# The last expert tile reaches the tokens by a matmul, the other tiles are gathered beside it, and x is stored in quarters

## What is computed

```python
# layer 0: top 1 of 8 experts, capacity int(512 / 8 * 1.25) + 1 = 81
slot = where(rank < capacity, top1 * capacity + rank, trash)
h = gelu(einsum('ecd,edf->ecf', eb, W1) + b1)
y = einsum('ecf,efd->ecd', h, W2) + b2
x = x + where(valid, y[slot], 0) * combine_w
# layer 1: top 2 of 8 experts, no capacity
for e in experts:
    w = sum(gates * (topi == e), -1)
    h = silu(x_ @ gate_w[e].T) * (x_ @ up_w[e].T)
    acc = acc + (h @ down_w[e].T) * w
x = x + acc          # x_ is the layer norm of x; out = x
```

## Time and profile before

| what | value |
|---|---|
| runs, us | 3772.26, 3777.95, 3777.58 (median 3777.58) |
| the profiled execution, us | 3774.2 |
| its span, us | 3772.9 |
| PE busy | 3586.1 us, 95% |
| DVE busy | 2570.7 us, 68% |
| ACT busy | 1928.2 us, 51% |
| POOL busy | 1774.7 us, 47% |
| experts of layer 0, first to last expert matmul | 1784.6 to 1978.3 |
| experts of layer 1, first to last expert matmul | 3225.7 to 3750.6 |

### The profile page before, as it was taken

The page is one execution under the profiler, slowest core; times in us unless marked ns, Lnnn a source line. Parts: engine busy times, 40 slices in busy tenths (PEclk is TensorE's granted clock), DMA queues, the critical chain, the costliest instruction groups (busy, mean ns, idle before and its releaser), DMA issues. The chain is left out here.

```text
span 3772.9 us, 46236 instructions
## 1 busy us (share of the span) xinstructions
PE 3586.1 (95%) x17924; PEld 2322.5 (62%) x17924; DVE 2570.7 (68%) x3488; ACT 1928.2 (51%) x1978; POOL 1774.7 (47%) x744
## 2 busy tenths in 40 slices
PE   8999999999999999988997999999999887999997
PEld 6788788655555555446873555555554475788886
DVE  3222344478878787546986787878775565899997
ACT  2122312366555555633981655555566322678775
POOL 2112112299999899700000989999998320100000
PEclk9999999999999999998996999999999998999999
DMA  7667765633333333045875333333330101899996
GB/s 280 201 201 237 240 207 195 203 78 86 89 77 88 90 84 74 20 149 191 358 316 161 75 86 79 81 90 90 77 88 23 51 1 44 346 380 374 371 379 249
DMA packets 235177, 613.76 MB, mean 163 GB/s; under 512 B 43169, under 2 KB 125121, under 8 KB 180689
## 3 DMA queue, kind: packets, MB, share of 16 engines
q1 hardware_dynamic: 196176, 537.40, 43.8%
q10 hardware_dynamic: 36864, 67.13, 4.8%
q0 software_dynamic: 1920, 6.29, 0.5%
HBM read 480.07 MB, written 130.58 MB: 162 GB/s over the span
## 5 line engine op out<-in xcount | busy, mean ns | idle before, releaser
L731 DVE TENSOR_REDUCE maxima<-psum 128x1 f32<-128x512 f32 x2048 | 1285.5, 682 | 341.6 <-PE psum L726 338.6
L840 ACT ACTIVATE pt<-psum 128x1024 f32<-128x1024 f32 x1024 | 1018.8, 1025 | 701.6 <-PE psum L751 696.1
L854 POOL TENSOR_TENSOR exp_sums<-pt 128x1024 f32<-128x1024 f32 x342 | 818.7, 2394 | 265.4 <-PE psum L767 131.5
L726 PE MATMUL psum<-ks,first_q 96*128 96x512 f32 x2048 | 814.3, 447 | 20.1 <-DMA first_q<-q_parts 10.1
L857 POOL TENSOR_TENSOR exp_sums<-exp_sums,pt 128x1024 f32<-128x1024 f32 x310 | 736.8, 2377 | 45.8 <-ACT pt L840 1.5
L726 PEld LDWEIGHTS psum<-ks,first_q 96*128 96x128 f32 x2048 | 393.9, 192 | 477.8 <-DVE maxima L731 323.7
L763 PE MATMUL psum<-pt,vs 128*32 128x512 f32 x4096 | 674.3, 598 | 4.6 <-DVE head_rows L868 2.3
L767 PE MATMUL psum<-exp_sums,constants 128*32 128x512 f32 x1408 | 670.2, 598 | 0.0
L751 PE MATMUL psum<-qs,ks 97*128 97x512 f32 x2048 | 649.4, 400 | 15.3 <-ACT pt L840 15.3
L1512 DVE TENSOR_TENSOR moe_cut<-moe_raw,moe_cut 128x2048 fp32r<-128x2048 f32 x244 | 557.3, 2290 | 57.0 <-ACT moe_cut L1508 51.4
L1508 ACT CAST moe_cut<-moe_raw 128x2048 fp32r<-128x2048 f32 x244 | 468.8, 1924 | 50.5 <-PE psum L97 47.8
(11 more groups left out here) (323 smaller groups left out, 4594.7 us busy)
## 6 DMA issues: line engine op xcount, KB each, us to landing
moe_raw<-in_moe_w SPq DMA_DIRECT2D x244, 1024.0 KB, 7.8
ks<-k_parts SPq DMA_DIRECT2D x384, 256.0 KB, 4.6
k_parts<-kparts ACTq DMA_DIRECT2D x256, 256.0 KB, 4.0
cx<-in_ctx SPq DMA_DIRECT2D x32, 1024.0 KB, 6.1
vs<-v_heads SPq DMA_DIRECT2D x32, 1024.0 KB, 5.2
v_heads<-vrow SPq DMA_DIRECT2D x28, 1024.0 KB, 5.1
late_context<-cparts SPq DMA_DIRECT2D x16, 512.0 KB, 12.2
late_parts<-late_context SPq DMA_DIRECT2D x16, 512.0 KB, 3.8
```

The source lines that it names most:

```text
L726: pe.matmul(self.c.bank[self.FIRST_BANK + k % 3], self.first_q[s][:, t * P:(t + 1) * P], self.ks[s][part][0:3 * DH, at:at + CHUNK], start= ...
L731: dve.tensor_reduce(self.maxima[:, h % 2, i % TT, i // TT:i // TT + 1], self.c.bank[self.FIRST_BANK + k % 3], X, ALU.max).then_inc(*self.f ...
L840: act.activation(self.pt[:, self.slot(h, b) + i:self.slot(h, b) + i + 2, :], self.c.psum[:, at:at + 2, :], ACT.Exp).then_inc(*self.exp.up())
L854: engine.tensor_tensor(to, self.pt[:, slot:slot + R, :], self.pt[:, slot + R:slot + 2 * R, :], ALU.add).then_inc(*signal.up())
```

## The change

- In tile 1, ahead of that tile's other work, DVE builds `spread`: for each of the four token tiles a 128x128 matrix with the token's weight at its place in the last tile, zero elsewhere (5 instructions in layer 0; 14 in layer 1, where a second matrix for the second choice is built in `select` and added).
- At the start of tile 2 PE transposes the four matrices into the bank of the turned tokens, and ACT copies them to `spread_t`.
- The last tile isn't stored to `y_slots`. Its rows there hold zeros, for which two more tiles of zeros are written early in the program (rows of tile 7, layer 0's last, and of tile 14, layer 1's last).
- POOL's gathers wait for the stores of the other tiles only, so they stand beside the last tile's work. DVE adds their rows ahead of the last tile's output in layer 0, behind its last operand work in layer 1.
- When the last tile's output is in `moe_yrow`, PE multiplies it by the four matrices, 128x512 each, into four banks, and DVE adds each to x.
- In layer 1 SP stores each quarter of x when it is ready. The wait for these stores stands ahead of the stage's barrier, not behind it.

```diff
@@ ProjectContext.loads_and_stores
-                for t in range(TT):
-                    sp.dma_start(S["y_slots"][(EXPERTS + t) * P:(EXPERTS + t + 1) * P, :], self.nothing[:]).then_inc(*self.zeros_out.up())
+                for tile in (EXPERTS - 1, *range(EXPERTS, EXPERTS + TT), TILES1 - 1):
+                    sp.dma_start(S["y_slots"][tile * P:(tile + 1) * P, :], self.nothing[:]).then_inc(*self.zeros_out.up())
@@ Experts
+    def spread_last_on_dve(self, dve):
+
+        for n in range(self.choices):
+            dve.tensor_scalar(self.place[:, n, :], self.slots[n], -float((self.tiles - 1) * P), None, ALU.add).then_inc(*self.placed.up())
+        dve.wait_ge(*self.placed.at(self.choices))
+        for t in range(TT):
+            dve.tensor_scalar(self.spread[:, t, :], self.c.iota[:], self.place[:, 0, t:t + 1], self.gate[0][:, t:t + 1], ALU.is_equal, ALU.mult).then_inc(*(self.placed if self.two else self.spread_made).up())
+        if self.two:
+            for t in range(TT):
+                dve.tensor_scalar(self.select[:, t, :], self.c.iota[:], self.place[:, 1, t:t + 1], self.gate[1][:, t:t + 1], ALU.is_equal, ALU.mult).then_inc(*self.spread_made.up())
...
+            for t in range(TT):
+                dve.tensor_tensor(self.spread[:, t, :], self.spread[:, t, :], self.select[:, t, :], ALU.add).then_inc(*self.spread_made.up())
@@ loads_and_stores
-        store(self.tiles - 1)
+        if self.out is not None:
+            for t in range(TT):
+                sp.wait_ge(*self.x_added.at(TT * self.choices + t + 1))
+                sp.dma_start(self.out[t * P:(t + 1) * P, :], self.x[:, t, :]).then_inc(*self.stored.up())
+            sp.wait_ge(*self.stored.all())
@@ on_pe, tile(j), at its start
+            if j == self.SPREAD_TILE:
+                pe.wait_ge(*self.spread_made.at(TT * self.choices))
+                for t in range(TT):
+                    last = pe.transpose(bank[self.X_BANK][:, t * P:(t + 1) * P], self.spread[:, t, :], c.ident[:])
+                last.then_inc(*self.spread_turned.up())
@@ on_pe, behind the last tile
+        pe.wait_ge(*self.y_done.at(self.tiles))
+        for t in range(TT):
+            pe.matmul(bank[t], self.spread_t[:, t, :], self.yrow[:, (self.tiles - 1) % 2, :], start=True, stop=True).then_inc(*self.last_made.up())
@@ on_act, at the start of a tile
+            if j == self.SPREAD_TILE:
+                act.wait_ge(*self.spread_turned.at(1))
+                act.copy(self.spread_t[:], bank[self.X_BANK].rearrange("p (t n) -> p t n", t=TT)).then_inc(*self.spread_copied.up())
@@ on_dve
+            if j + 1 == self.SPREAD_TILE:
+                self.spread_last_on_dve(dve)
...
+                if j + 1 == self.tiles:
+                    add_back()
                 dve.wait_ge(*self.used.at((j + 1) * self.pieces))
...
+        if self.two:
+            add_back()
+        for t in range(TT):
+            dve.wait_ge(*self.last_made.at(t + 1))
+            dve.wait_ge(*self.x_added.at((t + 1) * self.choices))
+            dve.tensor_tensor(self.x[:, t, :], self.x[:, t, :], bank[t], ALU.add).then_inc(*self.x_added.up())
@@ perceiver
-            nc.sync.dma_start(out.rearrange("(t p) d -> p t d", p=P), x[:]).then_inc(*stored.up())
-            nc.sync.wait_ge(*stored.all())
```

More of the change, by code:

```diff
@@ L1184, with __init__ @@
     AHEAD, RAW, CUT, JB = 3, 6, 4, FT // FB
-    EARLY_LOWS = 2
+    EARLY_LOWS, SPREAD_TILE = 2, 2
     TURN_BANK, X_BANK, OUT_BANK = 4, 6, 7
-    def __init__(self, c, A, S, x, l):
-        self.c, self.A, self.S, self.x, self.l = c, A, S, x, l
+    def __init__(self, c, A, S, x, l, out=None):
+        self.c, self.A, self.S, self.x, self.l, self.out = c, A, S, x, l, out
         self.two = l == 1
@@ L1206, in run @@
             self.select = c.sb(st, f"select{l}", [P, TT, P])
+            self.place = c.sb(st, f"place{l}", [P, 2, TT])
+            self.spread = c.sb(st, f"spread{l}", [P, TT, P])
+            self.spread_t = c.sb(st, f"spread_t{l}", [P, TT, P])
             self.norm = Normalize(c, st, self.x, f"ln_m{l}")
@@ L1237, in run @@
             self.first_ranked, self.selected = c.signals(st, "first_ranked selected")
+            self.placed, self.spread_made, self.spread_turned, self.spread_copied, self.last_made = c.signals(st, "placed spread_made spread_turned spread_copied last_made")
+            self.stored, = c.landings(st, "stored")
             if not self.two:
@@ L1283, in select_first_on_dve @@
             dve.tensor_scalar(self.select[:, t, :], self.c.iota[:], 1.0, self.first_rank[:, t:t + 1], ALU.add, ALU.is_equal).then_inc(*self.selected.up())
+    def spread_last_on_dve(self, dve):
[7 more added lines that the diff above has]
+                dve.tensor_scalar(self.select[:, t, :], self.c.iota[:], self.place[:, 1, t:t + 1], self.gate[1][:, t:t + 1], ALU.is_equal, ALU.mult).then_inc(*self.spread_made.up())
+            dve.wait_ge(*self.placed.at(self.choices + TT))
+            dve.wait_ge(*self.spread_made.at(TT))
+            for t in range(TT):
+                dve.tensor_tensor(self.spread[:, t, :], self.spread[:, t, :], self.select[:, t, :], ALU.add).then_inc(*self.spread_made.up())
     def plan_top1_on_dve(self, dve):
@@ L1321, in plan_top1_on_dve @@
         dve.tensor_copy(self.row_of[:, 0, :], slot).then_inc(*self.rows_known.up())
-        self.gate = [weight]
+        self.gate, self.slots = [weight], [slot]
     def plan_top2_on_dve(self, dve):
@@ L1382, in plan_top2_on_dve @@
         dve.tensor_copy(self.owneri[:], self.ownerf[:]).then_inc(*self.slot_made.up())
-        self.gate = [w1, w2]
+        self.gate, self.slots = [w1, w2], [slot1, slot2]
     def loads_and_stores(self, sp):
@@ L1497, in tile @@
                 if db == 1 and j + 1 < self.tiles:
+                    if j == self.SPREAD_TILE:
+                        pe.wait_ge(*self.spread_copied.at(1))
                     turn_x(j + 1)
@@ L1595, in leave_turned, with add_back @@
             dve.tensor_tensor(to, source, high.bitcast(F32), ALU.subtract).then_inc(*self.ht_low.up())
+        def add_back():
+            for t in range(TT):
+                dve.wait_ge(*self.y_back[t].at(self.choices))
+                for n in range(self.choices):
+                    if n:
+                        dve.wait_ge(*self.x_added.at(t * self.choices + n))
+                    dve.scalar_tensor_tensor(self.x[:, t, :], self.back(t, n), self.gate[n][:, t:t + 1], self.x[:, t, :], ALU.mult, ALU.add).then_inc(*self.x_added.up())
         for g in range(self.EARLY_LOWS, self.AHEAD):
@@ L1619, in on_dve @@
                 dve.tensor_tensor(self.yrow[:, j % 2, :], bank[self.OUT_BANK], self.bias2[:, j % 2, :], ALU.add).then_inc(*self.y_done.up())
+        if self.two:
+            add_back()
         for t in range(TT):
-            dve.wait_ge(*self.y_back[t].at(self.choices))
-            for n in range(self.choices):
-                if n:
-                    dve.wait_ge(*self.x_added.at(t * self.choices + n))
-                dve.scalar_tensor_tensor(self.x[:, t, :], self.back(t, n), self.gate[n][:, t:t + 1], self.x[:, t, :], ALU.mult, ALU.add).then_inc(*self.x_added.up())
+            dve.wait_ge(*self.last_made.at(t + 1))
+            dve.wait_ge(*self.x_added.at((t + 1) * self.choices))
+            dve.tensor_tensor(self.x[:, t, :], self.x[:, t, :], bank[t], ALU.add).then_inc(*self.x_added.up())
 def over_heads(mask):
@@ L2103, in perceiver @@
         DeltaRule(c, A, x).run()
-        Experts(c, A, scratch, x, 1).run()
-        with ExitStack() as st:
-            stored, = c.landings(st, "stored")
-            nc.sync.dma_start(out.rearrange("(t p) d -> p t d", p=P), x[:]).then_inc(*stored.up())
-            nc.sync.wait_ge(*stored.all())
+        Experts(c, A, scratch, x, 1, out).run()
 CONST_AT, CONST_COLS = {}, 0
```

## The result

The changed kernel takes **3754.91 us** (median of four runs, 3750.64 to 3762.04), the kernel before 3777.76 (four runs, 3772.26 to 3780.86). The ratio is **0.9946, 95% interval 0.9934 to 0.9958**: 20.4 us faster, 16 to 25 (the two medians lie 22.85 apart). The forecast was 3757 in a range of 3750 to 3766.

The account below looks back on a forecast made before the run. PE was taken to bound the tiles, and one short thing after another the tails, where PE idles. The terms, -6.4 - 14.3 + 0.9 + 1.1 = -18.7 us, from an average of 3775.5 gave 3757, range 3750 to 3766.

Parts of the forecast that it names:

- Tail of layer 0, -6.4: From layer 0's last output to the next stage: 5.18 us for 11.61, so 6.4 us saved.
- output to the fourth add, 4.1: In both tails, from the last output to the fourth new add: 0.05 signal, 7 x 0.43, and 1.05, making 4.1 us.
- 7 x 0.43 to the eighth weight load: In the four new matmuls, PE's eighth weight load was put seven intervals of 0.43 us behind the first.
- Tail of layer 1, -14.3: From layer 1's last output to the span's end, with x stored in quarters: 7.3 us for 21.6.
- Rival 3: At layer 1's end the quarter stores don't help: landing is 4.4 us again, -16.4 in all, 3759; chance 0.06.
- The gathers fit, 0: Beside the last tile in both layers, gathers and their adds finish in time and cost nothing; cover thin in layer 0, 1.7 us.
- the price of 2.2 us: If gathers beside DVE's low parts run slow, layer 1 loses 0.9 us and layer 0 1.3: sum 2.2 us worse.
- Rival 1: Gathers beside the last tile are late in both layers: 12.4 us less gain, -6.3, 3769; chance 0.05.
- Transposes, +0.9: Four PE transposes in each layer, 0.44 us per four, paid in full because PE has no gap: 0.9 us added.
- Build in layer 1, +1.1: In tile 1, DVE's 2.8 us build makes it 1.95 late; PE waits that less a 0.82 lead at the fourth product.
- Rival 4: DVE's lag in layer 1 never heals and recurs in 14 tiles: +19 at the full 2.8 us each, 3795; chance 0.02.
- Rival 2: The new matmuls in both tails run at half clock, 3.4 us more per layer: -11.9, 3764; chance 0.06.

Follow-up runs that it names:

- x_whole: The changed kernel with x stored by one DMA behind the barrier, as before; layer 1's tail 9.25 us, 2.4 longer than with quarters.
- build_doubled: The changed kernel with twelve more unread DVE operations behind the build in tile 1 of layer 1; tile 1 took 38.64 us, 3.09 longer.
- no_two_input_lows: The changed kernel with memsets for DVE's low parts in layer 1's last tile; all eight gathers took 0.94 to 0.98 us each.
- turned_five_times: The changed kernel with the four transposes done five times over in each layer; up to the output, layer 0 took 196.27 us, layer 1 529.32.
- build_shared_out: The changed kernel with layer 1's build dealt out over tiles 1 to 4 and turned in tile 6; 0.9949 of before, tile 1 35.01 us.

## Why the prediction was right

The time is 3754.91 for 3757, and the sum of its steps -20.3 by the stages for -18.7. The mechanism was the one forecast: the tails shrink because the gathers move beside the last tile, and PE pays a little in the middle. By its own steps:

- **Tail of layer 0, -6.4:** measured -6.75. One term, "output to the fourth add, 4.1" was over-sized: it is 1980.26 - 1976.47 = 3.79 (and 3.78 in layer 1). The 1.05 us from the last weight load to the add held; "7 x 0.43 to the eighth weight load" did not. Weight loads in layer 1, PEld, which answer to the earlier trace rows:

```profile
3742.04 0.30 PEld L1537 LDWEIGHTS psum<-moe_yrow,spread_t 128*128 128x128 f32 x2 [1.15 <-ACT moe_yrow L1604]
3742.58 0.19 PEld L1537 LDWEIGHTS psum<-moe_yrow,spread_t 128*128 128x128 f32 x1 [0.24 <-issue]
...
3744.72 0.19 PEld L1537 LDWEIGHTS psum<-moe_yrow,spread_t 128*128 128x128 f32 x1 [0.24 <-issue]
```

  The first two loads take 0.30 us together, so they start 0.11 apart; I take it that no matmul is under way yet that the second has to wait for. Only the six intervals behind them are 0.43, and the eighth starts 2.68 us behind the first, not 3.0. The add of 0.69 and the barrier of 0.39 held to 0.01.
- **Tail of layer 1, -14.3:** measured -14.8, 0.3 of it by the same term. The last quarter landed in 2.0, for the 2.1 taken from stores of line 1390, and the one DMA of 1024 KB took its 4.4 again in x_whole. The Trainium skill's page "DMA: Bandwidth & Descriptors", section "Anatomy of one DMA — SWDGE (gpsimd) path", gives an estimated 2.6 for a quarter; all four took 2.0 to 2.1 here, and only build_doubled, with up to 2.7, came near it. Rival 3 falls.
- **The gathers fit, 0:** right in the result, with less to spare than said. Their pace was put at 1.32 us with 3.26 as the slow bound; it is 15.0 / 7 = 2.14, for the cause that no_two_input_lows shows. That is 5.7 us more up to the last gather of layer 1. It cost nothing, because DVE took up its eight adds only at 3735.20, behind its last operand work, and ran them without a gap: each pair had landed when its turn came, and the last gathered add ended 0.9 us ahead of the output. The last gather, from 3735.80, landed 3.6 us later, 0.9 us ahead of its add. So the price of 2.2 us, reckoned for the slow pace, didn't come: the gathers were slow and it was hidden. Layer 0 has 2.12 us of DVE's idle time left. Rival 1 falls.
- **Transposes, +0.9:** 0.44 in each layer, shown by turned_five_times. In layer 0 it doesn't show in the sum (-0.04), for 0.4 us that came back and that no step had; its cause is open. The two more stores of zeros, put at 0, cost nothing: from 60 to 200 us, where they are issued, PE is busy for 140.00 of 140.00 us with them and without.
- **Build in layer 1, +1.1:** a wait of PE for the fourth hidden product was named, and it is there, once, with tiles 2 and up nearly at their old pace. Its size was half. DVE, then PE in tile 1 of layer 1, which answer to the earlier trace rows:

```profile
3252.01 0.23 DVE L1294 TENSOR_SCALAR place<-small 128x4 f32<-128x4 f32 x2
3252.28 1.12 DVE L1297 TENSOR_SCALAR spread<-constants,place,small 128x128 f32<-128x128 f32 x4
3253.32 1.11 DVE L1300 TENSOR_SCALAR select<-constants,place,small 128x128 f32<-128x128 f32 x4
3254.53 0.90 DVE L1304 TENSOR_TENSOR spread<-spread,select 128x128 f32<-128x128 f32 x4
3255.35 4.48 DVE L1547 TENSOR_TENSOR moe_cut<-moe_raw,moe_cut 128x2048 fp32r<-128x2048 f32 x2
3259.75 0.68 DVE L1622 TENSOR_TENSOR moe_h<-moe_h,psum 128x512 f32<-128x512 f32 x1
...
3275.95 0.68 DVE L1622 TENSOR_TENSOR moe_h<-moe_h,psum 128x512 f32<-128x512 f32 x1
...
3276.69 0.66 PE L1496 MATMUL psum<-constants,moe_h 128*128 128x128 f32 x4 [0.31 <-DVE moe_h L1622]
```

  The build is 3255.35 - 3252.01 = 3.34 us, not 2.8, and DVE's lag at the first product is 2.3 us, not 1.95. But by the fourth product, which stood 24.20 us behind tile 0's output before and stands 25.43 behind it now, it is 1.23: a DVE that is late runs its pairs of low parts in 4.48 instead of 4.62 and without the idle moments between. Less the lead of 0.82 that leaves 0.41; the wait shown is 0.31 and the tile is 0.55 longer. The forecast kept the lag constant over the tile ("PE waits there for 1.95 - 0.82"), though it gave this as the lower bound. build_shared_out shows the 0.55 to be the build's. With 0.44 for the transposes that makes 1.0 of the 1.29; the other 0.3 comes in small pieces that no step had (tiles 3, 5 and so on to 13 take 35.04, where they took 35.01 before), in build_shared_out too, and its cause is open. Rival 4, by which the lag never heals, falls: even after build_doubled the later tiles keep their time.
- **Clock:** full in both layers. Rival 2 falls.

That the whole times agree within 2.1 us is also some luck. The terms (tail of layer 0, tail of layer 1, layer 0 and layer 1 up to the output) were off by -0.35, -0.5, -0.5 and -0.25 us, all to the cautious side and together -1.6, and the whole time of one execution moves by more than that in stages that nobody touched. The forecast also started from 3775.5, while the median before, with its fourth run, is 3777.76.

## What to carry to other kernels

A chain of store, gather and add behind the last matmul is worth taking apart by what it waits for: most of it waited for data that had long been there, and one small matmul for the one part that had not let everything else move beside work. Added work that must stand beside a full PE is cheapest in portions that the idle time and the lead of its engine at that place can cover (0.94 and 1.54 us were free here); one lump of 3.34 us was paid as, roughly, the lag that was left at the product with the least lead, less that lead. Price such a lag at that product and not where it arises: it had shrunk from 2.3 to 1.2 us on the way. And where whole times vary by 0.2%, cut the traces at events that every version has: the experts' stages repeated within 0.1 us, but for the landing of the last store, and gave each term by itself.

## What the hardware did that was not expected

- POOL's issue of an indirect DMA is 0.94 to 0.98 us alone, beside memsets, or when it starts ahead of a DVE operation with two SBUF inputs. When it starts during one, it ends 0.8 us behind that operation's end, if that is later than its own 0.95 us: 2.0 to 2.9 us beside low parts of 2.29 us, 1.42 beside an add of 0.75 us.
- The same last DMA of 1024 KB from the same buffer landed in 4.4 us in two kernels and in 5.5 in a third; quarters of it in 2.0 to 2.1 in most traces and in up to 2.7 in build_doubled.
- Quarter stores issued among gathers took up to 4.6 us instead of 2.0, and the gathers beside them 4.6 to 5.8 instead of 3.5 to 3.8: cutting a store into pieces gained 2.4 us with nothing beside it and 1.1 with gathers beside it.
- The delta rule's stage, with the same 1080 matmuls, took 221.3 us at a mean granted clock of 0.92 and 228.1 at 0.88, from one execution to another; the stage up to the first tokens took 1781.6 to 1787.6 us at a mean granted clock of 0.98 in every trace, and the short experts' stage of layer 0 between them 194.5 each time.
